# An attention of sixteen heads taken batch by batch, with the routing of the first batch's experts placed among the later heads

## The reference

```python
q = l2norm(x @ w_q) * exp(scale)          # 16 heads of 64
k = l2norm(x @ w_k);  v = x @ w_v
x = layernorm(x + concat(softmax(q @ k.T) @ v) @ w_out + b_out)

top_v, top_i = top_k(x @ gate_w.T, 2)     # 8 experts, 2 of them for each token
p = softmax(top_v)
x = layernorm(x + sum_k p_k * ((silu(x @ wg[e_k].T) * (x @ wu[e_k].T)) @ wd[e_k].T))

# depthwise convolution of width 3, then a scan over the 1024 steps of a batch with 16 states
x = layernorm(x + scan(conv(x)))

# 8 experts again, 2 for each token, square(relu(.)), and one shared expert for all tokens
x = layernorm(x + experts(x) + shared(x))
```

## Time and profile before

| | us |
|---|---|
| median of three runs | 1067.99 |
| lowest and highest run | 1067.62, 1071.31 |
| the profiled execution, its own time | 1074.72 |
| its span, first to last instruction | 1072.9 |
| TensorE busy in the span | 914.0 (85%) |
| ScalarE busy | 769.8 (72%) |
| VectorE busy | 729.0 (68%) |
| GpSimd busy | 499.3 (47%) |

### The profile page before, as it was taken

The page is one execution under the profiler, slowest core; times in us unless marked ns, Lnnn a source line. Parts: engine busy times, 40 slices in busy tenths (PEclk is TensorE's granted clock), DMA queues, the critical chain, the costliest instruction groups (busy, mean ns, idle before and its releaser), DMA issues. The chain is left out here.

```text
span 1072.9 us, 34731 instructions
## 1 busy us (share of the span) xinstructions
PE 914.0 (85%) x13676; PEld 859.2 (80%) x13676; DVE 729.0 (68%) x1463; ACT 769.8 (72%) x1275; POOL 499.3 (47%) x385
## 2 busy tenths in 40 slices
PE   3889999999999999999999951899969579899930
PEld 2778998999989989989999841899969469899830
DVE  6699988988998898889889743432459759410202
ACT  5689998988999889989888640544465356598831
POOL 5475755564655555555646116512328170043423
PEclk8799999999999999999999965899999679899975
DMA  8300000000000000000000041313201012023211
GB/s 261 114 2 5 20 3 22 3 3 22 3 3 22 3 22 3 3 23 2 3 22 2 2 177 39 102 54 83 54 26 33 3 40 58 13 66 97 61 55 42
DMA packets 43131, 42.13 MB, mean 39 GB/s; under 512 B 5600, under 2 KB 37344, under 8 KB 42848
## 3 DMA queue, kind: packets, MB, share of 16 engines
q1 hardware_dynamic: 38880, 31.51, 9.7%
q0 software_dynamic: 4096, 8.40, 2.8%
HBM read 25.60 MB, written 14.29 MB: 37 GB/s over the span
## 5 line engine op out<-in xcount | busy, mean ns | idle before, releaser
L557 ACT ACTIVATE Pr<-SC,cur_nesc,cur_esc 128x1024 f32<-128x1024 f32 x256 | 309.9, 1211 | 33.8 <-PE SC L417 17.3
L654 DVE TENSOR_TENSOR Pl<-Pr 128x1024 f16<-128x1024 f32 x224 | 287.5, 1302 | 44.8 <-ACT Pr L557 43.0
L416 PE MATMUL SC<-QK 128*128 128x256 f16 x1024 | 238.8, 274 | 1.0 <-ACT QK L539 1.0
L417 PE MATMUL SC<-QK 128*128 128x256 f16 x1024 | 238.9, 274 | 0.0
L442 PE MATMUL OP<-V,Pr 128*128 128x65 f16 x2048 | 214.4, 192 | 5.9 <-DVE Ob L676 5.8
L444 PE MATMUL OP<-V,Pr 128*128 128x64 f16 x2048 | 215.2, 195 | 0.0
L446 PE MATMUL OP<-V,Pl 128*128 128x65 f16 x2048 | 214.0, 191 | 0.0
L442 PEld LDWEIGHTS OP<-V,Pr 128*128 128x128 bf16 x2048 | 191.0, 97 | 12.6 <-issue 8.2
L444 PEld LDWEIGHTS OP<-V,Pr 128*128 128x128 bf16 x2048 | 190.0, 97 | 2.5
L446 PEld LDWEIGHTS OP<-V,Pl 128*128 128x128 f16 x2048 | 190.6, 99 | 0.0
L789 POOL TENSOR_TENSOR stk<-nrm,stk 128x512 f16<-128x512 f32 x64 | 75.2, 1175 | 147.6 <-DVE stk L636 147.6
(11 more groups left out here) (191 smaller groups left out, 2176.6 us busy)
## 6 DMA issues: line engine op xcount, KB each, us to landing
ys<-yb SPq DMA_DIRECT2D x92, 64.0 KB
xg<-xs SPq DMA_DIRECT2D x12, 384.0 KB, 4.0
wst<-in_up SPq DMA_DIRECT2D x8, 512.0 KB
xs<-zero SPq DMA_DIRECT2D x2, 1472.0 KB
scratch<-in_up SPq DMA_DIRECT2D x1, 2304.0 KB, 8.4
wd<-in_wd SPq DMA_DIRECT2D x4, 576.0 KB, 10.9
wd<-in_wd SPq DMA_DIRECT2D x4, 512.0 KB
QK<-in_wqkv SPq DMA_DIRECT2D x4, 384.0 KB, 7.4
```

The lines of the kernel that those rows point to most:

```text
L416: eng.matmul(out, QK[:, b, 1, key:key + P], rhs, start=True, stop=False)
L417: mm = eng.matmul(out, QK[:, b, 2, key:key + P], rhs, start=False, stop=True)
L557: eng.activation(Pr[:, n % PB, :, :], SC[s % 2][:, :, :], ACT.Exp, bias=cur_nesc[:, b:b + 1], scale=cur_esc[:, b:b + 1]).then_inc(s_exps, 1)
L654: eng.tensor_tensor(Pl[:, n % PB, :, :].rearrange("p a b -> p (a b)"), pr, high(pr)[:, 1::2], ALU.subtract).then_inc(s_low_probs, 1)
```

## The change

*Attention.* A head's 16 slots now belong to one batch and two heads: `head_of` and `token_tile` give head and tokens for a slot. Pairs 0 to 3 do batch 0, pairs 4 to 7 batch 1, so that batch 0's residual is complete in pair 4. The scales of all heads are made once. In pair 5 (`NORM_I`) and pair 6 (`PLACE_I`) the norm, the transposes, logits, ranks and slots of batch 0 are put into the slots, a few instructions in each, through bank `M1`; the 16 scatters of batch 0 stand in slots 11 to 30 of pair 6 and 2 to 18 of pair 7. TensorE waits at the head of slot 22 of pair 5 and of slot 3 of pair 6 until VectorE has read the logits and the ranks out of `M1`. The constants of GpSimd are made in pair 2.

*The second block.* It begins with `load_offsets(0)` and `sorted_turn(0)`. Norm and route of batch 1 stand behind tiles 0, 1 and 2 (`TURN_0`, `CHOOSE_0`, `PLACE_0`), its scatters are paced by tiles from 5 on, its rows are loaded behind stores 19 to 22 instead of 14, 17, 20 and 22, and its offsets in four chunks in the tile loop. The last layer's weights are loaded in four parts behind stores 2, 4, 6 and 8 and split in tiles 20 to 27 (before in tiles 0 to 7).

The core of the diff:

```diff
+TB = NT // B
+TILES = 23
+NORM_I, PLACE_I = 5, 6
+EARLY_ROWS_AT = 7
+EARLY_TURN_AT = (16, 17)
+EARLY_LOGITS_AT = (18, 19, 20, 21)
+CONSTANTS_I = 2
+CONSTANTS_AT = (2, 3, 9, 11, 12, 14, 18)
+SCATTER_AT = ((11, 12, 14, 18, 19, 25, 27, 28, 30), (2, 3, 9, 11, 12, 14, 18))
...
+        def token_tile(h, v):
+
+            return TB * (h // TB) + v % TB
+
+        def head_of(h, v):
+
+            return 2 * (h % TB) + v // TB
...
+            def early(i, s):
+
+                h, sh = 2 * i + s // SLOTS, s % SLOTS
+                tp = before(tp_slot, sh + 1)
+                if i == NORM_I and s in EARLY_TURN_AT:
+                    n = EARLY_TURN_AT.index(s)
+                    m1_free(h + 1, tp, i, s, 1)
+                    eng.wait_ge(s_rows, 4 * n + 4)
+                    wait(eng, s_xT, n)
+                    for r in range(4):
+                        mm = eng.transpose(M1[:, P * r:P * r + P], t["x"][:, 4 * n + r, :], ident32[:, :])
+                    mm.then_inc(s_x_turned, 1)
+                if i == NORM_I and s in EARLY_LOGITS_AT:
+                    n = EARLY_LOGITS_AT.index(s)
+                    if n == 0:
+                        m1_free(h + 1, tp, i, s, 1)
+                        eng.wait_ge(s_xT, 2)
+                        eng.wait_ge(constants.s_loaded, 16 * 9)
+                    for k in (2 * n, 2 * n + 1):
+                        mm = eng.matmul(M1[:, E * k:E * k + E], xT0[k // 4][:, P * (k % 4):P * (k % 4) + P], t["gate"][:, :], start=True,
+                                        stop=True)
+                    mm.then_inc(s_logits, 1)
+                if (i, s) == (PLACE_I, 1):
+                    m1_free(h + 1, tp, i, s, 1)
+                    eng.wait_ge(s_mask, 1)
+                    eng.wait_ge(constants.s_made, 7)
+                    mask, n = t["mask"][:, 0, :], (TB + 1) * E
+                    eng.matmul(M1[:, 0:n], t["tri16"][:, :], mask, start=True, stop=False, skip_group_check=True)
+                    for k in range(1, TB + 1):
+                        mm = eng.matmul(M1[:, E * k:n], t["ones16"][:, :], mask[:, 0:n - E * k], start=False,
+                                        stop=k == TB, skip_group_check=True)
+                    mm.then_inc(s_ranks, 1)
...
+                if (i, s) == (NORM_I, 22):
+                    eng.wait_ge(s_logits_read, 1)
+                if (i, s) == (PLACE_I, 3):
+                    eng.wait_ge(s_ranks_read, 1)
...
+            def early(i, s):
+                if i == NORM_I and EARLY_ROWS_AT <= s < EARLY_ROWS_AT + TB:
+                    k = s - EARLY_ROWS_AT
+                    eng.wait_ge(s_nmr, 1)
+                    xk = t["x"][:, k, :]
+                    eng.activation(xk, xk, ACT.Identity, bias=nmr[:, k:k + 1], scale=rstd[:, k:k + 1]).then_inc(
+                        s_rows, 1)
+                if i == NORM_I and s in EARLY_TURN_AT:
+                    n = EARLY_TURN_AT.index(s)
+                    eng.wait_ge(s_x_turned, n + 1)
+                    eng.activation(xT0[n], M1[:, :], ACT.Copy).then_inc(s_xT, 1)
+                if (i, s) == (NORM_I, 24):
+                    eng.wait_ge(s_rows, TB)
+                    eng.activation(split[:, :, 0:D], t["x"][:, 0:TB, :], ACT.Copy).then_inc(s_split_high, 1)
+                if (i, s) == (NORM_I, 27):
+                    eng.wait_ge(s_differences, 1)
+                    eng.activation(ex[:, :], df[:, :], ACT.Exp).then_inc(s_exp, 1)
...
+            def early_choose(s):
+
+                if s == 21:
+                    eng.wait_ge(s_logits, len(EARLY_LOGITS_AT))
+                    eng.tensor_copy(lg[:, :, :], M1[:, 0:TB * E].rearrange("p (k e) -> p k e", e=E)).then_inc(
+                        s_logits_read, 1)
...
+            def early_place(s):
+
...
+                if s == 2:
+                    eng.wait_ge(s_ranks, 1)
+                    eng.tensor_copy(rank[:, :, :], M1[:, 0:(TB + 1) * E].rearrange("p (k e) -> p k e", e=E)).then_inc(
+                        s_ranks_read, 1)
+                    eng.wait_ge(s_first_weight, 1)
...
+            def early(i, s):
+                if i == CONSTANTS_I and s in CONSTANTS_AT:
+                    constants.gpsimd(eng, CONSTANTS_AT.index(s))
+                if (i, s) == (NORM_I, TB // 2 + 1):
+                    eng.wait_ge(s_ve, 1)
+                    eng.tensor_tensor(rstd[:, :], ve[:, :], half[:, 0:1].to_broadcast([P, TB]), ALU.pow).then_inc(
+                        s_rstd, 1)
+                if i in (PLACE_I, PLACE_I + 1) and s in SCATTER_AT[i - PLACE_I]:
+                    m = (i - PLACE_I) * len(SCATTER_AT[0]) + SCATTER_AT[i - PLACE_I].index(s)
+
+                    eng.wait_ge(s_exps, 2 * SLOTS * i + s)
+                    if m == 0:
+                        eng.wait_ge(s_slots, 1)
+                        eng.wait_ge(s_split_low, 1)
+                        eng.wait_ge(constants.s_cleared, 16 * B)
+                    eng.indirect_dma_start(
+                        out=t["xs"][0],
+                        out_offset=bass.IndirectOffsetOnAxis(ap=t["slots"][:, 0, m // TB, m % TB:m % TB + 1], axis=0),
+                        in_=split[:, m % TB, :], in_offset=None).then_inc(s_scattered, 16)
...
+TURN_0, CHOOSE_0, PLACE_0 = 0, 1, 2
+SCATTER_1 = 5
+LOAD_1_AT = {2: 0, 4: 1, 6: 2, 8: 3}
+LOW_AT = 20
...
-            eng.dma_start(stage, io["up1"]).then_inc(s_w1_loaded, 16)
-            for c in range(NC):
+            def load_weights(c):
+
                 cs = slice((E + 1) * P * c, (E + 1) * P * c + (E + 1) * P)
+                eng.dma_start(stage[:, cs], io["up1"][:, cs]).then_inc(s_w1_loaded, 16)
                 eng.dma_start(wd1[c][:, :], io["wd1"][:, cs]).then_inc(s_wd1_loaded, 16)
+
             for c in range(CHUNKS):
                 load(0, c)
             for j in range(TILES):
                 store(0, j)
-                if j in (14, 17, 20):
-                    load(1, (j - 14) // 3)
+                if j in LOAD_1_AT:
+                    load_weights(LOAD_1_AT[j])
+                if j in (19, 20, 21):
+                    load(1, j - 19)
             load(1, 3)
...
-                    if ph == 3 and j % CHUNK == 0:
+                    if ph in (1, 3) and j % CHUNK == 0:
...
-            turn(0, 0)
-            logits(0)
-            turn(0, 1)
-            logits(1)
-            ranks(0)
-            ranks(1)
             load_offsets(0)
-            load_offsets(1)
             sorted_turn(0)
             for u in range(SHARED_0 + LAG2):
                 if u + 1 < SHARED_0:
@@ -1213,6 +1463,12 @@
                     up_products(u)
                 if u >= LAG2:
                     down_products(u - LAG2)
+                if u == TURN_0:
+                    turn(0, 1)
+                if u == CHOOSE_0:
+                    logits(1)
+                if u == PLACE_0:
+                    ranks(1)
                 if u == TURN_1:
...
-            scatter(0)
-            scatter(1, -3)
+            scatter(1, SCATTER_1)
```

330 lines of the change are left out of this document (232 added, 98 removed).

## The result

| | before | changed |
|---|---|---|
| median, us | 1068.3 | 1056.93 |
| lowest and highest | 1067.62, 1071.31 | 1055.62, 1058.99 |
| the profiled execution's span | 1072.9 | 1054.8 |
| mean granted clock in it | 0.927 | 0.941 |

The account below looks back on a forecast made before the run. TensorE was taken as full but for some 48 us between attention and tiles, with little room on other engines before it. -42.5 + 7.3 + 4.7 + 4.8 + 13.2 = -12.5 us gave a median of 1055.5, range 1043 to 1067.

Parts of the forecast that it names:

- the two waits of the attention: TensorE waits for VectorE's bank reads at slot 22 of pair 5 and slot 3 of pair 6: 3.2 and 2.2 us.
- The gap: Between attention and expert tiles: the first tile starts 42.5 us earlier, after TensorE's four offset loads.
- First tiles: Batch 1's norm, logits and ranks behind tiles 0 to 2, at half clock, with 1.5 us waiting: +7.3 us.
- Offsets: Batch 1's weight offsets, loaded in TensorE's queue in the tiles: four chunks at 1.17 us each, +4.7 us.
- rows of tile 23: Load of batch 1's first rows, now behind store 19: TensorE waits uncovered before tile 23, +4.8 us.
- side remark: Before tile 23: an earlier row load would not help much, as sixteen scatters end about then too.
- The attention: Work put into attention's slots: TensorE +3.0, two waits +5.4, ScalarE +2.8, VectorE +2.0, in all +13.2 us.
- The order and the weights: Attention's order by batches and the last expert layer's later weight loads and splitting: each costs nothing.
- second rival: Pairs 5 and 6: ScalarE and VectorE become the bound; attention pays 23 us, total 1065.3; chance 0.20.
- Hidden: Rival: attention hides most of the added work and pays 5.5 us, total 1047.8; chance 0.19.
- ScalarE and VectorE bound: The second rival, in attention pairs 5 and 6: attention pays 23 us, total 1065.3; chance 0.20.
- GpSimd: Rival: slow scatters in attention hold up transposes, making GpSimd the bound; total 1071.5 to 1087.5; chance 0.07.

Follow-up runs that it names:

- e13_burst: Changed kernel with batch 1's sixteen scatters one after another, not one per tile; tiles 4 to 22 took 44.56 us against 45.40 in the changed kernel.
- e3_offsets: Changed kernel with all four loads of batch 1's weight offsets ahead of tile 23's transposes; 2.8 us less at the median.
- e1_loads: Changed kernel with batch 1's rows loaded behind stores 16, 18, 20 and 22 and its scatters paced from tile 2; 2.5 us less at the median.
- e2_waits: Changed kernel with logits in slots 18 and 19, read by VectorE in 19, and ranks read at the head of slot 2; 4.0 us less at the median.
- e6_order: Kernel before with only the order by batches and the scales of all heads taken from the change; ratio to the kernel before 0.9993.
- e9_all: Changed kernel with the edits of e1_loads and e2_waits, and batch 1's ranks and placing one tile later; ratio to the kernel before 0.9827.
- e10_best: e9_all with batch 1's scatters from tile 5, two per tile from tile 10, and batch 0's normalised rows a slot later; 3.7 us over e9_all.
- the ten: Ten runs in the first three experiment groups, beside which the kernel before had a median of 1075.0 to 1075.2 us.

## Why the prediction was right

Forecast 1055.5 (1043 to 1067), measured 1056.93: 12.5 us less had been forecast and 11.4 came. The two traces differ by 12.77 up to the turn, 11.3 without the slow tile in that of before. The large term and the two waits of the attention came as worked out. Three smaller terms hold as sums only, by errors that cancel. By its steps:

- **The gap, -42.5.** Measured -43.17. The first tile came 4.89 behind the block's start instead of 5.5. TensorE's offset loads set it, as forecast; the four lasted 1.01, 1.47, 0.85 and 1.23, 4.6 in sum, where four times the median had given 5.6.
- **First tiles, +7.3.** Measured +7.4 from tile 0 to tile 22. That the sum fits is luck. TensorE was not at half clock throughout: it rose at about 651, fell behind the mask's wait and rose again. So the logits cost 1.95 and not 3.58, 1.6 less, and the second fall of the clock, which the sum had not, cost 1.3 (e13_burst, where it did not come). The wait for the mask was 1.92, against 1.5.
- **Offsets, +4.7, and rows of tile 23, +4.8.** Together +9.06, or 10.5 without a single slow tile of 3.89 in the trace of before. A chunk cost 1.5 rather than 1.17, so the full load of 1.4 stands in TensorE's way, and for three chunks only; the first, behind the hole, cost some 0.7 (e3_offsets, which has no load there). The hole was 4.20 against 4.8, but the slow clock behind it cost more, which the sum had not: without the load the two intervals behind it take 6.09 where before has 4.94, so 1.2.
- **The reason given in a side remark there was wrong**: that an earlier load would not have helped much because the scatters end about then. The last scatter starts at 701.3, 7 us before the load is issued (708.27). e1_loads moved both and closed the hole, and e13_burst shows that the scatters were not holding it. How much an earlier load alone gives was not run.
- **The attention, +13.2.** Measured +13.95, or 13.6 to 13.9 by the exponentials. The two waits were 3.05 and 2.37, against 3.2 and 2.2; taking out 4.9 us of them gives 4.0 (e2_waits). That the clock would fall behind the first was not in the sum. The split of the rest was a guess that held in sum: 1.8 at slot 8 is ScalarE's wait for `nmr` and its rows, 1.7 more to slot 21 with the transposes and logits. What VectorE's share of it is was not tried apart.
- **The order and the weights, nothing.** e6_order: 0.9993. Tiles 6 to 15 run at 2.40 us, a little under the 2.46 of before; no run moves the weights alone.
- **The bounds.** Two sums of the prediction are not exact. The second rival with the upper bound of the route is 1065.3 + 2.7 = 1068, not 1067. The lower bound of the attention, 5.5, follows from no sum of its terms: it is 3.0 without the waits and 8.4 with them. Neither bears on the outcome.
- **The rivals.** "Hidden" and "ScalarE and VectorE bound" are 8 and 9 us away from what the attention paid. GpSimd: the scatters were slow, 1.78 us, as that rival supposed, and cost 0.5. "Wrong it would be if scatters amid the attention took 2 us" was a bad test: an engine's longer instruction is no price before it is shown who waits for it.
- **The profiled executions.** I carried the 6.7 us by which before's profiled run exceeded its median over to the changed kernel. Its own profiled run was not above its median; the difference of 18.1 in span is thus larger than that of the medians: 5.4 of it lies in a part that the change leaves as it was, and 1.45 in the slow tile.

What stays open: why TensorE pauses in e9_all, and ScalarE in e10_best's last layer, with nothing named that they await. Full DMA engines and scatters back to back were both present in e13_burst without a pause, and the DMA engines were nearly idle in e10_best's last layer with pauses. Both were seen among the ten only, and neither kernel was run beside e13_burst. Also open is why a profile of the ten takes some 5 us longer in the last part.
